# Two products of the MLP's second matrix moved in between the last products of its first, four places for turned blocks, and a reordered second batch

## The chip, the cores and the metric

The kernel runs on one core of a Trainium2 chip. Time is device microseconds of one execution; a kernel's time is the median of its runs. Engines: PE (TensorE, matmuls), DVE (VectorE), ACT (ScalarE), POOL (GpSimd), SP (SyncE, which only issues DMAs here). Every engine works through its own list of instructions in order, and waits on semaphores that the kernel sets by hand.

## The reference

A transformer block with cross attention, B = 4 batches of 512 tokens, D = 512, 16 heads of 32, hidden width 2048, all in fp32:

```python
x = layer_norm(hidden_states, ln1_w, ln1_b)
q = (x @ q_w + q_b); k = (encoder @ k_w + k_b); v = (encoder @ v_w + v_b)   # split into 16 heads
attn = softmax(q k^T * scale)
out = (attn @ v) @ cproj_w + cproj_b
hidden = out + residual
y = layer_norm(hidden, ln2_w, ln2_b)
y = gelu(y @ fc_w + fc_b, approximate=True)
y = y @ proj_w + proj_b
return hidden + y
```

## The kernel before, in words

A product in fp32 precision is made of three matmuls on rounded operands, in `mm3`: every operand is held as a high part (a rounded copy, made by ACT) and a low part (operand less high part, made by DVE or POOL).

The first some 400 us are projections and attention, and the change doesn't touch them. Then comes the MLP, in two halves q = 0 and q = 1, each of two batches (2q and 2q + 1). A half has three stages on PE:

- the **front**: for p = 0 to 7, `fc_first(q, p)` and `fc_second(q, p)`, six matmuls each. `fc_second(q, p)` waits for ACT's `copy_first(q, p)`, which takes the result of `fc_first` out of PSUM. For q = 0 the four blocks `cproj(3, c)` of attention's output projection (twelve matmuls each) stand in the front too;
- the **rest**: for p = 0 to 7, five products `fc_rest(q, p, which)` of six matmuls each, which = 6, 5, 7, 4, 3. They are the seven-product scheme of Strassen and Winograd over the 2 x 2 blocks of batches and halves of the hidden features, so results are put together by additions on DVE: `add_u2` after product 6, `add_u3` after 7, `add_c22` after 5, `add_c21` after 4, `add_c12` after 3. ACT then applies GELU to each with `gelu_rest`;
- the **second product**: `pj(n)`, twelve matmuls for each of 32 features n (32 for each half). Before `pj(n)`, ACT makes the high parts of the weights and of the hidden feature (`second_high(n)`, `hidden_high(n)`), and DVE their low parts (`second_low(n)`, `hidden_low(n)`).

The operands of the rest are prepared during the front. The second batch of a half goes through a normalisation and a turn: DVE turns four 128 x 512 blocks (`y_block(b, c)`) into the tile `turned(b, c)`, SP stores each with four DMAs to the DRAM tensor yt (`y_store`), and loads yt back (`y_load`). Then DVE (`y_affine`) or ACT (`y_scale`) apply weight and bias, DVE forms four differences (`block(q, n)`, 128 x 1024 elements), and five operands YQ[0] to YQ[4] are split: high parts by ACT (`block_high`), low parts by DVE for 0 to 2 (`block_low`) and by POOL for 3 and 4. The weights of the rest ("wr") are loaded, POOL makes their sums (`weight_sums`), ACT their high parts (`rest_high(q, p)`), DVE their low parts (`rest_low(q, p)`). These lie in three places that are used in turn, `rest(q, p)`; `second(n)` shares memory with them.

All orders are written out by hand. In the rest, ACT's and DVE's lists for feature p stand in one loop; for p = 7 they hold `add_c21(7)`, `add_c12(7)` and two `gelu_rest`, and behind the loop the preparation of n = 2, 3 and on. The lines that later parts name: L991 `copy_first`, L994 all GELUs, L1050 and L1052 `rest_high`, L1108 `block_high`, L1061 `second_high`, L1075 `hidden_high`; L1299 `y_affine`, L1295 `y_block`, L1401 `block`, L1405 `block_low`, L1385 and L1388 `rest_low`, L1417 `add_u2`, L1427 `add_u3`, L1440 `add_c21`, L1447 `add_c12`, L1458 `second_low`, L1453 `hidden_low`; L1668 the low parts on POOL; L432 `y_store`, L439 `y_load`, L409 `load_weights` on SP.

## Time and profile before

| | |
|---|---|
| median of 3 runs | 771.61 us (769.97 to 775.69) |
| profiled execution | 771.54 us, of which the span from first to last instruction is 769.7 |
| PE busy | 729.8 us, 95% of the span |
| DVE, ACT, POOL busy | 544.4, 401.5, 351.0 us |
| TensorE clock, mean | 0.993 of full |

The span is nearly all PE. What an engine list or a wait costs is therefore read from PE's idle stretches and from the stretches in which its granted clock is below 1.00, and from what released PE at the end of each idle stretch. Other engines' idle time costs nothing by itself.

### The profile page before, as it was taken

The page shows a single profiled execution, that of the slowest core. Times are in us where ns is not written, and L with a number is a line of the kernel's source. Part 1 is how long each engine was busy: PE and PEld are TensorE (multiplying, and loading weights), DVE is VectorE, ACT ScalarE, POOL GpSimd, SP SyncE. Part 2 cuts the span into 40 slices and gives each one's busy share as a digit, 9 for nine tenths or more (in the row PEclk, how much of TensorE's full clock was granted, in tenths as well). Part 3 has the DMA queues.
Part 4 walks back from the last instruction along what each step waited for, and adds up shares of the span by engine and source line. Part 5 has one row for each costly group of instructions (what it writes and reads, how often), then busy time and mean ns, then how long its engine had stood idle before and what let it go on. Part 6 is the DMA issues. An engine that isn't in the chain of part 4 may idle for free.

```text
span 769.7 us, 10364 instructions
## 1 busy us (share of the span) xinstructions
PE 729.8 (95%) x3568; PEld 497.8 (65%) x3568; DVE 544.4 (71%) x1071; ACT 401.5 (52%) x690; POOL 351.0 (46%) x241
## 2 busy tenths in 40 slices
PE   7999999989999999999999889999999989999998
PEld 5878886733344444344436768778777878868886
DVE  6773347788888888898695857677599457654474
ACT  4434241276766666666684635354556554454442
POOL 2644150078998788798574367000045167000030
PEclk9999999999999999999999989999999999999999
DMA  9756377597666784678836832134883452033362
GB/s 328 236 161 229 127 223 231 196 265 171 157 165 149 187 235 115 173 197 180 228 103 156 259 105 70 40 85 115 212 270 104 118 179 83 27 96 96 95 207 82
DMA packets 118196, 124.24 MB, mean 161 GB/s; under 512 B 41248, under 2 KB 66084, under 8 KB 118144
## 3 DMA queue, kind: packets, MB, share of 16 engines
q1 hardware_dynamic: 91888, 98.39, 45.1%
q10 hardware_dynamic: 26256, 25.19, 11.0%
q8 instruction: 28, 0.46, 0.3%
q14 instruction: 24, 0.20, 0.1%
HBM read 94.05 MB, written 29.37 MB: 160 GB/s over the span
## 4 chain that ended last, share of the span: by engine, by line
PE 75%; DVE 15%; ACT 5%; issue 3%; DMA 1%; SPq 1%; POOL 0%; ACTq 0%; DVEq 0%
PE ps L592 20%; PE ps L594 19%; PE ps L593 19%; DVE ps L1344 7%; PE ps L715 5%; PE ps L699 5%; PE ps L684 4%; PE ps L730 4%; DVE R L1546 2%; ACT Pt L960 1%; DVE BIG L1458 1%; DMA yt<-FU 1%; DVE mx L1344 1%; PE ps L652 1%; DVE R L1276 1%
## 5 line engine op out<-in xcount | busy, mean ns | idle before, releaser
L960 ACT ACTIVATE Pt<-ps 128x512 f32<-128x512 f32 x256 | 137.6, 597 | 72.4 <-PE ps L699 71.5
L699 PE MATMUL ps<-BIG 98*128 98x512 f32 x256 | 92.7, 439 | 3.5 <-ACT Pt L960 3.1
L1344 DVE CUSTOM_DVE_ANT_0 ps<-ps,FU 128x512 f32<-128x512 f32 x128 | 84.6, 722 | 14.9 <-PE ps L684 14.8
L1344 DVE CUSTOM_DVE_ANT_0 ps<-ps,BIG 128x512 f32<-128x512 f32 x128 | 84.6, 723 | 10.9 <-PE ps L684 10.7
L699 PEld LDWEIGHTS ps<-BIG 98*128 98x128 f32 x256 | 44.1, 188 | 67.5 <-issue 28.3
L1458 DVE TENSOR_TENSOR BIG<-RW,BIG 128x512 fp32r<-128x512 f32 x64 | 50.2, 784 | 49.4 <-ACT BIG L1061 49.3
L1061 ACT ACTIVATE BIG<-RW 128x512 fp32r<-128x512 f32 x64 | 40.3, 629 | 80.7 <-PE ps L594 79.8
L592 PE MATMUL ps<-BIG,HR 128*128 128x512 f32 x172 | 68.4, 397 | 5.2 <-DVE HR L1453 5.2
L994 ACT ACTIVATE BF<-BF,cols 128x512 f32<-128x512 f32 x48 | 34.5, 723 | 68.1 <-DVE BF L1447 29.5
L1800 POOL TENSOR_TENSOR R<-Pt 128x1024 f32<-128x1024 f32 x20 | 47.3, 2390 | 46.6 <-ACT Pt L960 46.6
L1739 POOL TENSOR_TENSOR R<-R,cbt 128x512 f32<-128x512 f32 x16 | 26.0, 1652 | 93.2 <-DMA R<-hd 93.2
L715 PE MATMUL ps<-Pt,V 128*32 128x512 f32 x512 | 68.2, 605 | 0.0
L593 PE MATMUL ps<-BIG,HR 128*128 128x512 f32 x172 | 67.5, 393 | 0.0
L594 PE MATMUL ps<-BIG,HR 128*128 128x512 f32 x172 | 67.5, 392 | 0.0
L1668 POOL TENSOR_TENSOR BIG<-R,BIG 128x512 fp32r<-128x512 f32 (+1 forms) x31 | 42.4, 1391 | 45.9 <-ACT BIG L972 27.0
L592 PE MATMUL ps<-BIG 128*128 128x512 f32 x128 | 52.7, 411 | 7.0 <-DVE BIG L1475 5.8
L1331 DVE SCALAR_TENSOR_TENSOR BIG<-ps,cols,BIG 128x512 fp32r<-128x512 f32 x31 | 23.0, 748 | 45.4 <-ACT BIG L942 45.2
L1800 POOL TENSOR_TENSOR RAWY<-Pt 128x1024 f32<-128x1024 f32 x22 | 52.1, 2389 | 3.9 <-ACT Pt L960 3.9
L942 ACT ACTIVATE BIG<-ps,cols 128x512 fp32r<-128x512 f32 x31 | 21.3, 688 | 57.4 <-PE ps L594 57.4
L592 PE MATMUL ps<-BIG,WK 128*128 128x512 f32 x128 | 50.9, 398 | 0.0
L593 PE MATMUL ps<-BIG 128*128 128x512 f32 x128 | 50.8, 397 | 0.0
L594 PE MATMUL ps<-BIG 128*128 128x512 f32 x128 | 50.5, 395 | 0.0
(186 smaller groups left out, 1734.9 us busy)
## 6 DMA issues: line engine op xcount, KB each, us to landing
RW<-in_proj_w ACTq DMA_DIRECT2D x64, 256.0 KB, 2.6
BIG<-qs SPq DMA_DIRECT2D x62, 256.0 KB, 2.8
BIG<-ks SPq DMA_DIRECT2D x62, 256.0 KB, 3.1
ks<-BIG SPq DMA_DIRECT2D x32, 256.0 KB, 2.0
qs<-BIG SPq DMA_DIRECT2D x32, 256.0 KB, 5.5
R<-hd SPq DMA_DIRECT2D x20, 256.0 KB, 4.1
RW<-in_fc_w ACTq DMA_DIRECT2D x20, 256.0 KB, 3.0
R<-in_x SPq DMA_DIRECT2D x16, 256.0 KB, 5.4
```

Of the source, the lines that this page charges most:

```text
L592: eng.matmul(outp, a[0], b[0], start=first, stop=False, skip_group_check=onto)
L593: eng.matmul(outp, a[1], b[0], start=False, stop=False, skip_group_check=onto)
L594: return eng.matmul(outp, a[0], b[1], start=False, stop=last, skip_group_check=onto)
L699: eng.matmul(bk, K_[0:98, j, kc * 128:(kc + 1) * 128], Q_[0:98, j, :], start=True, stop=True).then_inc(S["p_ra"], 1)
L715: ins = eng.matmul(bank(7)[32 * j:32 * j + 32, :], V[:, 4 * b + kc, c:c + 32], Pt[:, r, j % 2, :], start=kc == 0, stop=kc == 3)
L960: eng.activation(Pt[:, r, j % 2, :], bank(bank_a(("s2", i, j))), ACT.Exp, scale=SCALE).then_inc(S["a_ra"], 1)
L994: eng.activation(dst, src, ACT.Gelu_apprx_tanh, bias=fcb[:, f:f + 1]).then_inc(S[done], 1)
L1061: eng.activation(second(n)[0], raw_w(("pj", n, 0)), ACT.Copy).then_inc(S["a_pj"], 1)
L1344: eng.tensor_tensor_reduce(out=scores, in0=scores, in1=MASK[s // 4], scale=1.0, scalar=-3.4e38, op0=ALU.add, op1=ALU.max, accum_out=mx[:, ...
L1458: eng.tensor_tensor(lo, raw_w(("pj", n, 0)), hi.bitcast(F32), ALU.subtract).then_inc(S["v_pj"], 1)
L1668: eng.tensor_tensor(dst, src, high.bitcast(F32), ALU.subtract).then_inc(S[name], 1)
L1800: eng.tensor_tensor(pair(m)[:, 2 * hp:2 * hp + 2, :], Pt[:, (r - 2) % 6, :, :], Pt[:, r, :, :], ALU.add).then_inc(S["g_ac"], 1)
```

## The change

It has five parts.

1. On PE, `pj(32q)` and `pj(32q + 1)` stand inside the last step p = 7 of the rest, where products 6, 5 and 7 of the next feature would stand: `pj(0)` before product 4, `pj(1)` between products 4 and 3. The first feature behind the rest is `pj(2)`. ACT's and DVE's preparation of these two is moved up to step p = 6, and the loads of their weights ahead of that step's GELUs.
2. In the front of q = 0, `cproj(3, 0)` and `cproj(3, 1)` move from step p = 2 to step p = 3.
3. `y_store(1)` and `y_load(1)` go ahead of the loads of wr 0 and wr 1 in SP's list. On DVE `y_affine(1)` and the four `block(0, n)` move up (p = 1 and 2 in place of p = 2, 3 and 4), and ahead of two `front_low_part`; on ACT the `block_high` and `rest_high(0, 0)`, `rest_high(0, 1)` move up.
4. In q = 1 the loads of wr 8 and wr 9 come with steps p = 0 and 1 of the front in place of 3 and 4, and `rest_high(1, 0)`, `rest_high(1, 1)` follow the GELUs of p = 5 and p = 7. `second(n)` for n from 32 on lies in other places.
5. `turned(b, c)` uses four places for batches 1, 2 and 3 (two in FU, two in R0), where batches 2 and 3 used the two of FU. So `y_block(3, c)` waits for the store of block c of batch 2, and no `y_block` waits for a store of its own batch.

```diff
-            return R0[:, c % 2, :] if b == 1 and c >= 2 else FU[:, c % 2, :]
+            return R0[:, c % 2, :] if b and c >= 2 else FU[:, c % 2, :]
...
             load_weights(("wf", 7, 0))
-            for m in range(2):
-                for h in range(2):
-                    load_weights(("wr", m, h))
             for c in range(4):
                 y_store(1, c)
             y_load(1)
-            for h in range(2):
-                load_weights(("wr", 2, h))
+            for m in range(3):
+                for h in range(2):
+                    load_weights(("wr", m, h))
...
+                    if q == 0 and p == 3:
+                        pe.wait_ge("v_rb", NB)
+                        for c in range(2):
+                            cproj(3, c, range(4), bank(c)).then_inc(S["p_cp"], 1)
                     fc_second(q, p)
-                    if q == 0 and 2 <= p < 4:
-                        pe.wait_ge("v_rb", NB)
-                        for c in (2 * p - 4, 2 * p - 3):
+                    if q == 0 and p == 3:
+                        for c in range(2, 4):
                             cproj(3, c, range(4), bank(c)).then_inc(S["p_cp"], 1)
...
                     if p + 1 < HF:
                         fc_rest(q, p + 1, 6)
+                    else:
+                        pj(32 * q)
                     fc_rest(q, p, 4)
                     if p + 1 < HF:
                         fc_rest(q, p + 1, 5)
+                    else:
+                        pj(32 * q + 1)
                     fc_rest(q, p, 3)
                     if p + 1 < HF:
                         fc_rest(q, p + 1, 7)
-                for n in range(32 * q, 32 * q + 32):
+                for n in range(32 * q + 2, 32 * q + 32):
                     pj(n)
...
-                if b == 1 and c >= 2:
-                    dve.wait_ge("p_sm", NS)
-                elif c >= 2:
-                    dve.wait_ge(f"d_ys{c - 2}", 64 * (b + 1))
+                if b == 3:
+                    dve.wait_ge(f"d_ys{c}", 64 * b)
                 elif b == 2:
                     dve.wait_ge("v_wr", 2 * HF)
-                elif b:
-                    dve.wait_ge(f"d_ys{c + 2}", 64 * b)
+                elif b == 1 and c >= 2:
+                    dve.wait_ge("p_sm", NS)
+                elif b == 1:
+                    dve.wait_ge(f"d_ys{c + 2}", 64)
+                elif c >= 2:
+                    dve.wait_ge(f"d_ys{c - 2}", 64)
```

**The end of the rest on ACT.** These are ACT's rows before, from the loads of the weights of `pj(2)` and `pj(3)` on. L994 are GELUs; behind the one that waits for s_v_c12 the second time come `second_high(1)` and `second_high(2)`.

```order
L1081 DMA RW<-in_proj_w 128x512 [waits s_v_wr]
L1081 DMA RW<-in_proj_w 128x512
L994 ACTIVATE BF<-BF,cols 128x512 [waits s_v_c22]
L1061 ACTIVATE BIG<-RW 128x512 [waits s_p_p3,s_d_w0]
L1075 ACTIVATE HR<-BF 128x512 [waits s_a_g11]
L994 ACTIVATE BF<-BF,cols 128x512 [waits s_v_c21]
L994 ACTIVATE BF<-BF,cols 128x512 [waits s_v_c12]
L1061 ACTIVATE BIG<-RW 128x512 [waits s_d_w1]
L1075 ACTIVATE HR<-BF 128x512 [waits s_a_g11]
L1061 ACTIVATE BIG<-RW 128x512 [waits s_d_w2]
L1075 ACTIVATE RX<-BF 128x512 [waits s_a_g11]
```

And after, at the same place:

```order
L1000 ACTIVATE BF<-BF,cols 128x512 [waits s_v_c21]
L1067 ACTIVATE BIG<-RW 128x512 [waits s_p_p3,s_d_w0]
L1081 ACTIVATE HR<-BF 128x512 [waits s_a_g11]
L1000 ACTIVATE BF<-BF,cols 128x512 [waits s_v_c12]
L1000 ACTIVATE BF<-BF,cols 128x512 [waits s_v_c22]
L1067 ACTIVATE BIG<-RW 128x512 [waits s_d_w1]
L1081 ACTIVATE HR<-BF 128x512 [waits s_a_g11]
L1000 ACTIVATE BF<-BF,cols 128x512 [waits s_v_c21]
L1000 ACTIVATE BF<-BF,cols 128x512 [waits s_v_c12]
L1067 ACTIVATE BIG<-RW 128x512 [waits s_d_w2]
L1081 ACTIVATE RX<-BF 128x512 [waits s_a_g11]
```

The preparation of features 0 and 1 moved ahead of the last two GELUs; that of feature 2 (the last two rows) still stands behind both.

**The front of q = 0 on DVE**, before, from the load of batch 1 on:

```order
L1299 TENSOR_SCALAR BF<-BF,cols 128x512 [waits s_d_yl3]
L1379 TENSOR_TENSOR RY<-RW,RY 128x512 [waits s_a_wf]
L1601 TENSOR_TENSOR R<-ps,R 128x512 [waits s_g_xc,s_p_cp] x2
L1401 TENSOR_TENSOR BF<-BF,HN 128x1024 [waits s_p_ra,s_v_ya]
L1401 TENSOR_TENSOR BF<-BF 128x1024 [waits s_v_tt]
L1601 TENSOR_TENSOR R<-ps,R 128x512 [waits s_g_xc,s_p_cp] x2
L1401 TENSOR_TENSOR BF<-BF 128x1024
L1401 TENSOR_TENSOR BF<-HN,BF 128x1024 [waits s_v_tt]
L1405 TENSOR_TENSOR SLX<-BF,SLX 128x1024 [waits s_a_yq] x2
L1385 TENSOR_TENSOR BIG<-V,BIG 128x256 [waits s_a_wr]
L1388 TENSOR_TENSOR BIG<-FU,BIG 128x1024 [waits s_a_wr]
L1405 TENSOR_TENSOR SLX<-BF,SLX 128x1024 [waits s_a_yq]
```

And after:

```order
L1305 TENSOR_SCALAR BF<-BF,cols 128x512 [waits s_d_yl3]
L1407 TENSOR_TENSOR BF<-BF,HN 128x1024 [waits s_p_ra,s_v_ya]
L1407 TENSOR_TENSOR BF<-BF 128x1024 [waits s_v_tt]
L1385 TENSOR_TENSOR RY<-RW,RY 128x512 [waits s_a_wf]
L1407 TENSOR_TENSOR BF<-BF 128x1024
L1407 TENSOR_TENSOR BF<-HN,BF 128x1024 [waits s_v_tt]
L1385 TENSOR_TENSOR RY<-RW,RY 128x512 [waits s_a_wf]
L1610 TENSOR_TENSOR R<-ps,R 128x512 [waits s_g_xc,s_p_cp] x2
L1411 TENSOR_TENSOR SLX<-BF,SLX 128x1024 [waits s_a_yq] x2
L1610 TENSOR_TENSOR R<-ps,R 128x512 [waits s_g_xc,s_p_cp] x2
L1411 TENSOR_TENSOR SLX<-BF,SLX 128x1024 [waits s_a_yq]
L1391 TENSOR_TENSOR BIG<-V,BIG 128x256 [waits s_a_wr]
```

The four differences (L1401, now L1407) moved ahead of the additions of attention's output (L1601, now L1610) and of two low parts of front weights (L1379, now L1385, of which one stood ahead of these rows before).

## Rows read from the trace of the kernel before

**Rows 1.** The page, part 1: busy us, share of the span, instructions.
```profile
PE 729.8 (95%) x3568; PEld 497.8 (65%) x3568; DVE 544.4 (71%) x1071; ACT 401.5 (52%) x690; POOL 351.0 (46%) x241
```

**Rows 2.** PE's waits from 400 us on: total us, times, longest us.
```profile
PE ps L592 <- DVE HR L1453: 5.2, 6, 2.7
PE ps L592 <- DVE BF L1417: 2.8, 1, 2.8
PE ps L592 <- DVE BIG L1388: 2.3, 1, 2.3
PE ps L592 <- ACT BF L991: 1.9, 1, 1.9
PE ps L592 <- DVE BF L1427: 1.6, 2, 0.8
PE ps L592 <- POOL BIG L1668: 1.3, 1, 1.3
```

**Rows 3.** Windows: us, busy of PE, PEld, DVE, ACT, POOL, granted clock, DMA share, GB/s.
```profile
445.00:448.00 3.00, 1.04 (x3) 0.89 (x4) 1.81 (x2) 0.00 (x0) 3.00 (x4) 0.71 0.34 130
448.00:451.00 3.00, 3.00 (x9) 2.35 (x8) 1.00 (x2) 0.00 (x0) 2.92 (x5) 0.50 0.00 0
451.00:454.00 3.00, 3.00 (x10) 2.38 (x9) 1.07 (x2) 1.98 (x3) 0.78 (x2) 0.65 0.48 139
...
559.00:561.00 2.00, 2.00 (x5) 1.61 (x6) 1.95 (x2) 0.91 (x2) 1.54 (x2) 0.50 0.81 177
561.00:563.00 2.00, 2.00 (x8) 1.57 (x7) 2.00 (x3) 0.00 (x0) 1.43 (x1) 0.67 1.18 186
```

**Rows 4.** Timeline of ACT, two features apart by one: start, us, ..., idle before, releaser.
```profile
540.12 0.63 ACT L1061 ACTIVATE BIG<-RW 128x512 fp32r<-128x512 f32 x1 [1.57 <-PE ps L594]
...
542.84 0.63 ACT L1061 ACTIVATE BIG<-RW 128x512 fp32r<-128x512 f32 x1 [1.57 <-PE ps L594]
```

**Rows 5.** Timeline of DVE where the rest of q = 0 ends.
```profile
503.74 0.68 DVE L1447 TENSOR_TENSOR BF<-ps,BF 128x512 f32<-128x512 f32 x1
...
506.35 0.68 DVE L1453 TENSOR_TENSOR HR<-BF,HR 128x512 fp32r<-128x512 f32 x1
```

**Rows 6.** Timeline of ACT at the same place.
```profile
504.48 0.71 ACT L994 ACTIVATE BF<-BF,cols 128x512 f32<-128x512 f32 x1
```

**Rows 7.** Timeline of PE: q = 0's first product 7, and `pj(1)`.
```profile
446.95 0.77 PE L592 MATMUL ps<-SLX,BIG 128*128 128x512 f32 x1 [2.83 <-DVE BF L1417]
...
507.09 0.50 PE L592 MATMUL ps<-BIG,HR 128*128 128x512 f32 x1 [0.81 <-DVE HR L1453]
```

**Rows 8.** Timeline of SP, `y_store(1)` and `y_load(1)`.
```profile
408.67 6.45 SPq L432 DMA_DIRECT2D yt<-FU  x8
415.17 4.40 SPq L432 DMA_DIRECT2D yt<-R  x8
421.07 2.06 SPq L439 DMA_DIRECT2D BF<-yt  x4
```

**Rows 9.** Timeline of DVE in the front of q = 0.
```profile
424.01 2.84 DVE L1299 TENSOR_SCALAR BF<-BF,cols 128x512 f32<-128x512 f32 x3 [6.58 <-DMA BF<-yt]
...
429.45 1.21 DVE L1401 TENSOR_TENSOR BF<-BF,HN 128x1024 f32<-128x1024 f32 x1
...
443.42 2.79 DVE L1388 TENSOR_TENSOR BIG<-R,BIG 128x1024 fp32r<-128x1024 f32 x1 [0.52 <-ACT BIG L1052]
```

**Rows 10.** Timeline of ACT in the front of q = 0: `copy_first(0, 7)`.
```profile
439.09 0.60 ACT L991 ACTIVATE BF<-ps 128x512 f32<-128x512 f32 x1
```

**Rows 11.** Timeline of POOL there: low parts of YQ[3] and YQ[4].
```profile
439.28 5.84 POOL L1668 TENSOR_TENSOR YT<-BF,YT 128x1024 fp32r<-128x1024 f32 x2 [11.83 <-ACT YT L1108]
```

**Rows 12.** Timeline of DVE at the third block of batch 3.
```profile
557.06 0.71 DVE L1295 STREAM_TRANSPOSE FU<-R 128x512 f32<-128x512 f32 x1 [6.82 <-DMA yt<-FU]
```

**Rows 13.** Timeline of ACT at the end of q = 1's front: `rest_high(1, 0)`, `rest_high(1, 1)`.
```profile
618.96 0.42 ACT L1050 ACTIVATE BIG<-V 128x256 fp32r<-128x256 f32 x1 [0.30 <-issue]
...
621.11 1.04 ACT L1052 ACTIVATE BIG<-R 128x1024 fp32r<-128x1024 f32 x1
```

More of the change, by code:

```diff
@@ L110, in second @@
         def second(n):
-            return [BIG[:, 21504 + 1024 * (n % 3) + 512 * h:][:, 0:512] for h in range(2)]
+            base = (21504, 22528, 23552)[n % 3] if n < 32 else (19968, 21504, 18944)[n % 3]
+            return [BIG[:, base + 512 * h:][:, 0:512] for h in range(2)]
         SUMS = [t.rearrange("p a n -> p (a n)") for t in (FU, R0[:, 0:2, :])]
@@ L1220, in _ @@
                             load_weights(("wr", HF * q + p + 4, h))
+                    if 5 <= p < 7:
+                        load_weights(("pj", 32 * q + 2 * p - 10, 0))
+                        load_weights(("pj", 32 * q + 2 * p - 9, 0))
                     gelu_rest(q, p, 21)
+                    if p == 6:
+                        second_high(32 * q)
+                        hidden_high(32 * q)
                     gelu_rest(q, p, 12)
@@ L1230, in _ @@
                     if p == 6:
-                        second_high(32 * q)
-                        hidden_high(32 * q)
-                second_high(32 * q + 1)
-                hidden_high(32 * q + 1)
+                        second_high(32 * q + 1)
+                        hidden_high(32 * q + 1)
                 for n in range(2, 32):
@@ L1593, in _ @@
                         front_low_part(0, p + 4)
-                    if q == 0 and p == 2:
+                    if q == 0 and p == 1:
                         for k in range(4):
                             y_affine(1, k)
+                    if q == 0 and 1 <= p < 3:
+                        block(0, 2 * p - 2)
+                        block(0, 2 * p - 1)
                     if q == 0 and 3 <= p < 5:
@@ L1621, in _ @@
                         rest_low(q, p + 2)
+                    if p == 6:
+                        second_low(32 * q)
+                        hidden_low(32 * q)
                     add_c12(q, p)
@@ L1625, in _ @@
                         add_c22(q, p + 1)
[L1626 to L1628 removed]
+                    if p == 6:
+                        second_low(32 * q + 1)
+                        hidden_low(32 * q + 1)
                 for n in range(2, 32):
```

39 lines of the change are left out of this document (13 added, 26 removed).

## The prediction

> **What bounds the kernel now.** I read the page first: PE is busy for 729.8 of 769.7 us [rows 1]. The change adds no matmul and takes none away, so all it can move is PE's idle time and the stretches at the lower clock. Second, PE's waits in the MLP [rows 2]: they sum to 15.1 us in the six rows (a total of 16.1 with two of 0.6 and 0.4 that are left out). Each row belongs to one place. 1.3 is `cproj(3, 0)` waiting for POOL; 1.9 the last `fc_second` of q = 0 waiting for `copy_first`; 2.8 the first product 7 of the rest waiting for `add_u2`; 2.3 the start of the rest of q = 1 waiting for `rest_low`; 1.6 (twice 0.8) is product 4 of step 7 waiting for `add_u3`; of the 5.2 on `hidden_low`, 2.7 stands at feature 19 of q = 0, and most of the rest at the two hand-overs from the rest to the second product. Third, the granted clock [rows 3]. It is 1.00 but for two stretches: 0.71, 0.50 and 0.65 over 445 to 454 us, and 0.50 and 0.67 over 559 to 563. The lower level is 1.2 GHz, half of 2.4. A mean of 0.71 over 3 us is 1.74 us at half clock, so the first stretch holds 1.74 + 3.0 + 2.1 = 6.8 us, of which PE was busy 1.04 + 3 + 2.1 = 6.1 and lost half, 3.1 us. The second holds 2.0 + 1.3 = 3.3 us and lost 1.7. The first began in the idle of 2.8, the second in that of 2.7; idles of 2.3 and 1.9 had no such stretch. So the whole stock for this change is 16.1 + 3.1 + 1.7 = 20.9 us, 2.7% of the time.
>
> The unit: ACT's step to the next feature is released by PE every 542.84 - 540.12 = 2.72 us [rows 4], so `pj(n)` (twelve matmuls) takes 2.72 us and a product of six 1.36.
>
> **Part 1, `pj` inside the rest (twice, for q = 0 and 1).** What it removes: product 4 of step 7 no longer follows at once on product 7, whose result `add_u3` needs, so the 0.8 goes [rows 2]. The two idles at `pj(0)` and `pj(1)`, 0.3 and 0.8 (the second in [rows 7]), go or shrink: their operands are now made during step 6. Laying the same durations along step 6, I get `hidden_low(1)` some 0.3 us after PE wants `pj(1)`, an estimate. So 1.9 us of idle becomes 0.3.
>
> What it adds: behind product 3 of step 7 there is now nothing ready for PE. `pj(2)` needs `hidden_low(2)`, and this stands behind product 3 in every list: DVE's next is `add_c12(7)`, which reads product 3; ACT's next is the GELU on it; then `second_high(2)`, `hidden_high(2)`, then DVE's two low parts. The trace has the same chain for `pj(1)`: `add_c12` starts at 503.74 [rows 5], its GELU at 504.48 [rows 6], `hidden_low` at 506.35 [rows 5], and PE goes on at 507.09 [rows 7], 3.35 us after the start of the addition. Before, `pj(0)` with its 2.72 us covered most of it. Now nothing does: with some 0.2 us from product to addition PE stands still for 3.35 + 0.2 = 3.55 us (3.4 as the wait view counts, from the drain of the last matmul). Queued behind the waiting instructions are only the preparations of features 3 and on. Balance of one hand-over: each idle costs PE about 0.3 us more than the view counts, for the drain and the slower first matmul (0.50 for some 0.39 [rows 7]). Before, three idles: 1.9 + 0.8 = 2.7. Now two: 3.55 + 0.3 + 0.2 = 4.0. So +1.3 us. Bounds: 0 (if the addition came through at once and `pj(1)` didn't wait) and 2.
>
> Then the clock. An idle of 3.4 us is longer than both that were followed by half clock [rows 2, 3]. What it costs is bounded by 0 (as after 2.3) and by 3.1 us (as after 2.8); between the two stretches of before, 1.7 and 3.1, weighted for a chance that none comes, I take 1.9. Part 1 for both halves: 2 x (1.3 + 1.9) = +6.4 us, ends 0 and +10.
>
> **Part 5, four places.** DVE sat 6.8 us until a store of yt had landed before it could turn the third block of batch 3 [rows 12], and feature 19 waited behind that: 2.7 us idle [rows 2] and 1.7 at half clock. With four places the block waits for a store of batch 2, issued some 10 us earlier. What is late next there? DVE has 3 operations of 0.6 us for a feature of 2.72, and was some 3 us ahead of PE before that wait, so nothing is. Value: -2.7 - 1.7 = -4.4. Ends: -4.5 and -1 (POOL's low parts of batch 2, which slow DVE shortly after, could now catch it there).
>
> **Part 4, the start of q = 1's rest.** PE waited 2.3 us for `rest_low(1, 0)`, behind `rest_high(1, 0)`, which started at 618.96 [rows 13]. The weights are now loaded three steps of 2.72 us earlier and `rest_high(1, 0)` stands behind the GELU of step 5 in place of that of step 6, so this wait goes. But `rest_high(1, 1)` still follows the last GELU: it would end some 0.9 us earlier than the 622.15 of before [rows 13], and `add_u2` stands behind `rest_low(1, 1)` in DVE's list, so product 7, third of the rest, now waits some 1.4 us where it didn't. Value -1.0, ends -1.6 and 0. The moved loads stand ahead of two loads of front weights in ACT's list, which are needed two steps later, 5 us; four issues of some 0.5 us don't use that up.
>
> **Parts 2 and 3, the front of q = 0.** `cproj` behind a product more: the 1.3 us for POOL is hidden [rows 2]. SP issues the stores of yt in 6.45 us for the first eight, with 1 MB of wr ahead of them in the queues, and 4.40 for the next eight [rows 8]. Without it 16 cost 8.8 us and not 10.9, so `y_load(1)` goes out at 418.8 rather than 421.07, and `y_affine` starts near 421.7 rather than 424.01 [rows 9]. The blocks then end at about 431 rather than 435. On ACT three `block_high` fall before `copy_first` of step 7 as before, and `rest_high(0, 1)` (1.3 us) is added before it. I get its start at 438.1 for 439.09 [rows 10], so the last `fc_second` gains 1 us, no more: PE idles 2 us here as before. From there 6, 5 and 7 of step 0 need `rest_low(0, 0)` and `rest_low(0, 1)`. DVE's work from the last `y_affine` (425.1) to `rest_low(0, 1)` is 14.9 us: four `block` and three `block_low` of 1.2 [rows 9], two low parts and four additions of 0.6, two `rest_low` of 1.55. With no disturbance it is done at 440.0, PE flows from 438.8 on, product 7 starts at 442.9 rather than 446.95 [rows 7], and the clock doesn't fall: -4.05 - 3.1 = -7.1 us.
>
> But DVE is disturbed. The `rest_low` at 443.42 took 2.79 us where the same form takes 1.2, and it ended 1.1 us after POOL's second low part, which ended at 445.12 [rows 9, 11]. Before, POOL's two low parts, 2.9 us each, started at 439.28, when DVE had only `rest_low(0, 1)` left. Now `block_high` of YQ[3] ends at 433.5 on ACT, and POOL's 5.8 us fall over `block_low(0, 1)`, `block_low(0, 2)` and `rest_low(0, 0)`; its weight sums fall over the blocks. Each such meeting cost DVE 1.6 us in the row, and four to five of them make DVE 3 to 7 us late: product 6 starts at 441.5 to 445, product 7 at 444.3 to 447.8. I take 445.0, -2.0 us. PE then idles 2 us before the last `fc_second` and about as much before product 6, which makes the lower clock likely again: of the 3.1 us I count one back. Value -3.0; ends -7.1 and +3 (product 7 at 447.8 and 2 us more at half clock).
>
> The Trainium skill, page "SBUF — State Buffer", section "Who interferes with whom" and the diagram's reading before it, calls the port that VectorE and GpSimd share an exclusive lock, held for the whole instruction when the VectorE operation has two SBUF inputs. The row at 443.42 agrees. By the rule every low part and block here waits for a whole POOL instruction, by a sharing of bandwidth it would be slower by a part; the first gives the later end of my range for this part, the second about -5.
>
> **Sum.** +6.4 - 4.4 - 1.0 - 3.0 = -2.0 us on the profiled execution's 771.54 us (span 769.7 and 1.8 around it), which stands at the median, 771.61. Forecast: 769.5 us.
>
> **Rivals.** A: DVE isn't held up by POOL in the front. For it: 0.6 us operations pass between POOL's in many places. Against: the row of 2.79. Then the front gives -7.1: 771.5 + 6.4 - 4.4 - 1.0 - 7.1 = 765.4. B: the idle of 3.4 us leaves the clock alone, as 2.3 did; with the rest as forecast 769.5 - 3.8 = 765.7, and with A 761.6. Against it speak both stretches of [rows 3]. C, slower: DVE's lateness in the front. If `rest_low(0, 0)` comes later than 444, product 7 of step 0 starts later than before and PE's idle before product 6 is over 3 us, with half clock behind it: +3 there, and with both hand-overs at the 3.1 us price (2 x 4.4 = +8.8) the sum is +3 + 8.8 - 4.4 - 1.0 = +6.4, 777.9 us. It decides from about two meetings of DVE and POOL of full length more than I count. D: the hand-over costs nothing because the chain is shorter than in [rows 5 to 7]; I see no instruction that leaves it. It would give 769.5 - 6.4 = 763.1.
>
> **How the numbers follow.** Forecast 0.50, A 0.17, B 0.12, C 0.13, D and mishaps 0.08. Measurement can tell about 1%, 7.7 us. Range: 763 to 776, the forecast's own being 766.5 to 772.5. Faster by over 1% (below 763.9) needs A with B, or D: 0.19. Slower by over 1% (above 779.3) needs more than C: 0.06. Within: 0.75.
>
> **What would show it.** Right: PE idle of about 3.4 us before `pj(2)` and `pj(34)`, released by `hidden_low`; no wait of DVE on a store of yt near 557; a short wait at product 7 of q = 1. In the front, the start of product 7 of step 0 against 446.95 tells A, the forecast and C apart, and the length of DVE's L1411 and L1394 tells whether POOL is the cause. The granted clock behind each hand-over tells B. I am wrong if the hand-over shows under 2 us of idle, or if the third block of batch 3 still holds DVE.

## The result, and the profile after

The changed kernel takes 777.19 us (median of 13 runs, 774.32 to 780.06), the kernel before beside it 771.88 (13 runs). The ratio is 1.0067, with a 95% interval of 1.0047 to 1.0087: some 5.2 us slower. The forecast was 769.5 with a range of 763 to 776, and 777.19 lies above it. It lies 0.7 us from rival C's 777.9; whether C was right is taken up near the end.

The profiled execution of the changed kernel took 780.01 us (span 778.2, mean clock 0.987), 2.8 above its median, so its rows show more loss than the runs do. The line of the page that answers [rows 1]:

```profile
PE 734.9 (94%) x3568; PEld 501.5 (64%) x3568; DVE 548.2 (70%) x1071; ACT 401.5 (52%) x690; POOL 354.9 (46%) x241
```

The same 3568 matmuls take 5.1 us more, nearly all of it clock (worked out below), and PE's idle time rises from 39.9 to 43.3 us. PE's waits from 400 us on (total, times, longest), to set beside [rows 2]:

```profile
PE ps L591 <- DVE HR L1459: 5.6, 3, 3.4
PE ps L591 <- DVE BIG L1394: 3.8, 1, 3.8
PE ps L591 <- DVE RX L1459: 3.4, 1, 3.4
PE ps L591 <- ACT BF L997: 3.3, 2, 2.9
PE ps L591 <- DVE BF L1423: 1.3, 1, 1.3
PE ps L591 <- DVE RY L1385: 1.2, 1, 1.2
```

18.6 us in six rows, for 15.1 before. PE's timeline says where each stands (in brackets the idle time before the row):

```profile
442.01 0.50 PE L591 MATMUL ps<-YT,RY 128*128 128x512 f32 x1 [2.87 <-ACT BF L997]
447.45 0.79 PE L591 MATMUL ps<-SLX,BIG 128*128 128x512 f32 x1 [3.79 <-DVE BIG L1394]
...
512.97 0.79 PE L591 MATMUL ps<-BIG,RX 128*128 128x512 f32 x1 [3.38 <-DVE RX L1459]
...
586.54 0.50 PE L591 MATMUL ps<-BIG,HR 128*128 128x512 f32 x1 [1.96 <-DVE HR L1459]
...
628.97 0.47 PE L591 MATMUL ps<-SLX,BIG 128*128 128x512 f32 x1 [1.26 <-DVE BF L1423]
...
690.18 0.79 PE L591 MATMUL ps<-BIG,HR 128*128 128x512 f32 x1 [3.39 <-DVE HR L1459]
```

In order: the last `fc_second` of q = 0; product 6 of its rest, which waits for `rest_low(0, 0)`, where before product 6 went through and product 7 waited [rows 7]; `pj(2)`; `pj(27)`; product 7 of q = 1; `pj(34)`. The last row of the wait view, 1.2 us, is new and not in the forecast: at 435.89 us PE waits for a low part of the front's weights (L1385), ahead of which part 3 had put DVE's differences. The wait at feature 19 [rows 2] is gone, as is the 2.3 us before the rest of q = 1. A first matmul of 0.79 us in place of 0.50 ran at half clock already: the clock had fallen inside the idle. Windows of the two hand-overs (the seventh number is the granted clock):

```profile
513.00:516.00 3.00, 3.00 (x7) 2.42 (x8) 3.00 (x6) 1.28 (x3) 0.00 (x0) 0.50 0.32 109
516.00:519.00 3.00, 3.00 (x9) 2.28 (x9) 1.11 (x2) 0.45 (x1) 0.00 (x0) 0.53 0.00 0
...
693.00:696.00 3.00, 3.00 (x9) 2.33 (x8) 0.00 (x0) 0.24 (x1) 0.00 (x0) 0.50 0.00 0
```

Read in short windows, the clock stood at 1.2 GHz for 20.5 us: 6.8 at each hand-over (from 512.0 and 689.5, 1.0 and 0.7 us before the idle ended), 3.4 from 447.1, 3.4 from 587.1. Before it was 10.2 us [rows 3]. Half clock costs only while PE works: it was busy in 18.5 of the 20.5 us, and in 9.5 of the 10.2 before. Half of the difference is 4.5 us, most of the 5.1 by which PE's busy time grew.

**A ledger.** Taking the starts of the same DVE instruction in both profiles and subtracting gives the place of each loss. The first row is noise: attention has the same code in both, and over all twenty profiles of this study that point lay anywhere within 2.3 us.

| stretch | shift, us | forecast |
|---|---|---|
| up to 404 us, code unchanged | +0.9 | |
| front of q = 0, to `add_c12(0)` | +0.9 | -3.0 |
| first hand-over, to feature 8 | +4.0 | +3.2 |
| features 19 to 22 (four places) | -4.6 | -4.4 |
| features 22 to 28 | +3.4 | 0 |
| start of q = 1's rest | -0.2 | -1.0 |
| second hand-over, to feature 40 | +4.1 | +3.2 |
| all | +8.5 | -2.0 |

So the two hand-overs came as forecast or dearer, the four places gave what was forecast and lost most of it a few features later, and the front lost where it should have gained. One profile can't settle terms of one or two us, since half clock comes and goes between executions; the runs below can.

### The profile page after: what moved, and what is told of

It reads as the page before. It is cut to its first block, busy times and chain, and to the rows that moved or that the text cites. A ratio compares the mean times of both kernels' runs of the same rounds, so it can differ in the third digit from the quotient of the medians.

```text
span 778.2 us, 10363 instructions
## 1 busy us (share of the span) xinstructions
PE 734.9 (94%) x3568; PEld 501.5 (64%) x3568; DVE 548.2 (70%) x1071; ACT 401.5 (52%) x690; POOL 354.9 (46%) x241
## 4 chain that ended last, share of the span: by engine, by line
PE 73%; DVE 15%; ACT 4%; issue 3%; DMA 2%; SPq 1%; POOL 1%; ACTq 0%; DVEq 0%
PE ps L591 19%; PE ps L593 19%; PE ps L592 19%; DVE ps L1350 5%; PE ps L698 4%; PE ps L714 4%; PE ps L683 4%; PE ps L729 3%; DVE R L1552 2%; ACT Pt L966 1%; SPq L433 1%; DVE BF L1407 1%; DMA qs<-BIG 1%; PE ps L651 1%; DVE mx L1350 1%
## 5 line engine op out<-in xcount | busy, mean ns | idle before, releaser
L1350 DVE CUSTOM_DVE_ANT_0 ps<-ps,FU 128x512 f32<-128x512 f32 x128 | 84.6, 724 | 15.2 <-PE ps L683 15.1
L591 PE MATMUL ps<-BIG,HR 128*128 128x512 f32 x172 | 69.6, 405 | 5.8 <-DVE HR L1459 5.6
L593 PE MATMUL ps<-BIG,HR 128*128 128x512 f32 x172 | 68.7, 399 | 0.0
L592 PE MATMUL ps<-BIG,HR 128*128 128x512 f32 x172 | 68.7, 399 | 0.0
L1808 POOL TENSOR_TENSOR R<-Pt 128x1024 f32<-128x1024 f32 x20 | 47.3, 2386 | 45.8 <-ACT Pt L966 45.8
L1676 POOL TENSOR_TENSOR BIG<-R,BIG 128x512 fp32r<-128x512 f32 (+1 forms) x31 | 42.3, 1382 | 46.4 <-ACT BIG L978 27.0
L1337 DVE SCALAR_TENSOR_TENSOR BIG<-ps,cols,BIG 128x512 fp32r<-128x512 f32 x31 | 23.0, 749 | 45.9 <-ACT BIG L948 45.8
```

What stands on the lines that cost most here:

```text
L591: eng.matmul(outp, a[0], b[0], start=first, stop=False, skip_group_check=onto)
L592: eng.matmul(outp, a[1], b[0], start=False, stop=False, skip_group_check=onto)
L593: return eng.matmul(outp, a[0], b[1], start=False, stop=last, skip_group_check=onto)
L1350: eng.tensor_tensor_reduce(out=scores, in0=scores, in1=MASK[s // 4], scale=1.0, scalar=-3.4e38, op0=ALU.add, op1=ALU.max, accum_out=mx[:, ...
L1676: eng.tensor_tensor(dst, src, high.bitcast(F32), ALU.subtract).then_inc(S[name], 1)
L1808: eng.tensor_tensor(pair(m)[:, 2 * hp:2 * hp + 2, :], Pt[:, (r - 2) % 6, :, :], Pt[:, r, :, :], ALU.add).then_inc(S["g_ac"], 1)
```

## Each part by itself

Where the runs allow, a part is priced by its ratio to the kernel before, timed on the same chip.

**Part 1 taken out (e1).** The changed kernel with both preparations and both products back in their old places:

```diff
-                    else:
-                        pj(32 * q)
...
-                    else:
-                        pj(32 * q + 1)
...
-                for n in range(32 * q + 2, 32 * q + 32):
+                for n in range(32 * q, 32 * q + 32):
```

> The changed kernel without part 1: products pj(0), pj(1), pj(32), pj(33) and their preparation stand where they stood before, parts 2 to 5 stay. Theory H (the hand-over from the rest to the second product costs about 4 us each time, 1.3 of stall and nearly 3 of half clock, and parts 2 to 5 together are worth about nothing): 769 to 772 us, 0.997 to 1.001 of the kernel before, no idle over 2 us of PE at either hand-over. Rival P (only the stall, 1.3 us twice, belongs to the hand-over; the rest of the loss comes from parts 2 to 5): 774 to 775 us, 1.003 to 1.005.

771.47 us, ratio 0.9997 (0.998 to 1.0014). Theory H holds: what was lost goes away with part 1, and parts 2 to 5, forecast at -8.4 us together, are worth 0.2, give or take 1.3.

**Part 1 alone (e2)**, the opposite edit on the kernel before.

> The kernel before with part 1 alone (and the other places of second(n) in q = 1, which part 1 needs there). Theory H: PE idle of 3.4 us in front of pj(2) and pj(34), each with some 6.8 us at half clock behind it, 777 to 780 us, 1.006 to 1.010 of the kernel before. Rival P (stall alone): 774 to 775 us, 1.003 to 1.005.

777.76 us, ratio 1.0081 (1.0055 to 1.0106), +6.3 us; the forecast's term was +6.4. Its timeline of PE has both idles:

```profile
509.74 0.80 PE L593 MATMUL ps<-BIG,RX 128*128 128x512 f32 x1 [3.39 <-DVE RX L1459]
...
689.38 0.50 PE L593 MATMUL ps<-BIG,HR 128*128 128x512 f32 x1 [3.39 <-DVE HR L1459]
```

Half clock followed both here too, 3.4 us each, not 6.8 as in the changed kernel's profile and as the expectation had it.

**Part 5 alone (e3)**:

```diff
-            return R0[:, c % 2, :] if b == 1 and c >= 2 else FU[:, c % 2, :]
+            return R0[:, c % 2, :] if b and c >= 2 else FU[:, c % 2, :]
...
```

(The part left out is DVE's new waits, as in the diff ahead of the prediction.)

> The kernel before with part 5 alone. Theory G (most of the gain is given back a few features later, since the load of batch 3's yt comes no earlier and ACT's y_scale(3) stands ahead of second_high(24)): the idle of 2.7 us before pj(19) goes and another of 1.5 to 3 us comes at pj(24) or pj(25); 769.5 to 771.5 us, 0.997 to 1.000. Rival (the prediction's part 5, nothing is late next): 767.2 us, 0.994, and no idle between pj(16) and pj(26).

772.26 us, ratio 1.0001 (0.9982 to 1.0019): nothing of the 4.4 us. PE's idle at feature 19 is gone, and `pj(22)`, counted from the start of `pj(8)`, comes 4.5 us earlier, here and in every kernel of the study that has part 5. So the forecast's gain was there; but two other idles stand behind it, at features 24 and 27:

```profile
571.42 0.50 PE L592 MATMUL ps<-BIG,HR 128*128 128x512 f32 x1 [1.78 <-DVE HR L1455]
...
581.84 0.50 PE L592 MATMUL ps<-BIG,HR 128*128 128x512 f32 x1 [1.95 <-DVE HR L1455]
```

SP's and ACT's timelines say why for the first. SP of the kernel before, then of e3:

```profile
548.98 13.09 SPq L432 DMA_DIRECT2D yt<-FU  x16
563.86 2.70 SPq L439 DMA_DIRECT2D R<-yt  x4
```

```profile
548.87 7.23 SPq L432 DMA_DIRECT2D yt<-FU  x8
556.14 6.15 SPq L432 DMA_DIRECT2D yt<-R  x8
565.35 1.76 SPq L439 DMA_DIRECT2D R<-yt  x4
```

The blocks are turned earlier (the third at 549.85, before at 557.06), but SP still needs 13.4 us to issue their sixteen stores and the load goes out no sooner. Why SP takes as long when nothing waits for the blocks stays open. So ACT, now ahead by the 4.5 us gained, waits for that load, with `second_high(24)` behind it in its list. ACT's row in the kernel before, then in e3:

```profile
568.01 1.52 ACT L1085 ACTIVATE R<-R,cols 128x512 f32<-128x512 f32 x2 [0.45 <-DMA R<-yt]
```

```profile
568.00 1.52 ACT L1085 ACTIVATE R<-R,cols 128x512 f32<-128x512 f32 x2 [5.26 <-DMA R<-yt]
```

The same instruction starts at the same time in both; before, it had 0.45 us to wait, and that was all the room that there was. The second idle, at feature 27, falls together with POOL's `bias_add`; e14 and e17 below take it up.

**Parts 2 and 3 alone (e4)**, the edits as in the diff ahead of the prediction.

> The kernel before with parts 2 and 3 alone (the front of q = 0). Theory F (what the earlier blocks gain is lost to the meetings of DVE with POOL and to the later weights): product 7 of step 0 starts at 446 to 449 us, where it was 446.95, and the time is 771 to 773.5 us, 0.999 to 1.002. Rival (the prediction's parts 2 and 3): 768.8 us, 0.996, product 7 at 445.

772.63 us, ratio 1.0015 (0.9996 to 1.0034), +1.2 us. The rival, the forecast's own -3.0, is out. The time came as theory F had it, the place did not: what starts at 446.3 is product 6, and product 7, expected at 446 to 449, came at 450.4.

**Part 4 alone (e9)**:

```diff
-                    if q and 3 <= p < 5:
+                    if q and p < 2:
...
-                    if q and p == 6:
+                    if q and p == 5:
                         rest_high(1, 0)
```

> The kernel before with part 4 alone (and the other places of second(n) in q = 1). Theory Q (the idle of 2.3 us at the start of q = 1's rest goes, one of 1.3 us comes at product 7, and the half clock that followed the longer idle in five of seven profiles goes with it): 769 to 771 us, 0.997 to 0.999 of the kernel before. Rival (the prediction's 1.0 us is all given back at product 7): 771.5 us, 1.000.

769.93 us, ratio 0.9983 (0.9965 to 1.0002), -1.3 us, forecast -1.0. The interval leaves out a gain over 2.7 us, not zero. Over all profiles of the study, half clock followed the idle of 2.3 to 3.0 us at this place in 8 of 13 kernels without part 4, and the idle of 1.2 to 1.8 in none of 7 with it. The stall itself hardly shrank: from the start of the front of q = 1 to product 5 of step 2 of its rest PE takes 38.0 us in e9, and 38.05 in the kernel before, whose profile has no half clock there. Over the seven kernels with part 4 it is 37.7 to 38.1, but for e18; over the five without it whose profiles have no half clock at the start of the rest, 38.05 to 38.8. So by the profiles part 4 is worth some 0.4 us of stall, and the rest of the 1.3 is half clock that comes less often.

The four measured prices, +6.3, +0.1, +1.2 and -1.3, sum to +6.3 us, against 5.2 measured for the whole, which is within their intervals (each is 1.4 to 2 us either way).

## Why the hand-over costs that

**e5, one product inside, one behind product 3:**

```diff
                     if p + 1 < HF:
                         fc_rest(q, p + 1, 5)
-                    else:
-                        pj(32 * q + 1)
...
-                for n in range(32 * q + 2, 32 * q + 32):
+                for n in range(32 * q + 1, 32 * q + 32):
```

> The kernel before with part 1 changed: only pj(0) and pj(32) stand inside the rest, pj(1) and pj(33) follow product 3; the preparation of both is early as in part 1. Theory H (the chain from product 3 to hidden_low(2), 3.55 us, has nothing in front of it in part 1): the 2.72 us of pj(1) stand over it, the idle before pj(2) is 0.7 to 1.0 us, the idles before product 4, pj(0) and pj(1) are gone, no half clock at either hand-over; 768 to 770 us, 0.996 to 0.998 of the kernel before. Rival L (the early preparation on ACT and DVE is what costs, by delaying the GELUs and additions): 774 us or more, like part 1 alone.

767.45 us, ratio 0.9942 (0.9928 to 0.9957), a little better than even theory H had it. From e2 this is one product of each half moved by one place, and some 10 us less. PE's idle before `pj(2)` is what the chain is longer than `pj(1)`:

```profile
506.97 0.50 PE L593 MATMUL ps<-BIG,RX 128*128 128x512 f32 x1 [0.67 <-DVE RX L1457]
```

3.39 - 2.72 = 0.67 to the hundredth, and no half clock followed either hand-over.

**e6, the preparations early, PE's order as before** (both products behind product 3).

> The kernel before with ACT's and DVE's lists of part 1, while PE keeps its old order (all products pj behind product 3). Theory H: the idles before pj(0) and pj(1) go (0.3 and 0.8 us with the drain, twice), that of 0.8 before product 4 stays: 769 to 770.5 us, 0.997 to 0.999. Rival L (the lists are what costs): 774 us or more.

768.56 us, ratio 0.9952 (0.9935 to 0.9969), again below the case of theory H. The early lists cost nothing, they are the gain of part 1; rival L is out. With the same lists of ACT and DVE, e2, e5 and e6 differ only in which products PE has left when product 3 is done, and that is what costs.

**e7, stall against clock** (an edit of e2):

```diff
+                for _ in range(2):
+                    product(bank(FRONT_BANKS[q][0]), [x[:, 0:256] for x in rest(q, 7)], YQ[4], (0, 1), True)
                 for n in range(32 * q + 2, 32 * q + 32):
```

> The kernel before with part 1, and behind each product 3 of step 7 twelve more matmuls, 2.72 us, whose operands are ready and whose result nobody reads (a repetition of product 3 into a free bank), so that PE stands still for some 0.7 us in place of 3.4. The time to pj(2) is the same. Theory C (the clock falls because PE stands still, and that is the larger half of the hand-over's cost): no half clock behind either hand-over, 773.5 to 775.5 us, where part 1 alone gave 777.8. Rival S (the stall is the whole cost, the half clock would come somewhere in any case): 777 to 778.5 us.

775.35 us, ratio 1.0048 (1.0031 to 1.0064), 2.4 us under e2, though it does more work and `pj(2)` waits for the same chain. Its windows at the hand-overs:

```profile
509.00:512.00 3.00, 2.79 (x12) 2.30 (x13) 3.00 (x6) 1.43 (x3) 0.00 (x0) 1.00 0.46 130
688.00:691.00 3.00, 2.89 (x12) 2.36 (x13) 2.46 (x5) 1.41 (x3) 0.00 (x0) 1.00 0.33 120
```

Theory C holds in direction: without the half clock the same stall costs less. By the medians, 2.4 of the 6.3 us are clock and 3.9 are left for the stall, but other stretches of these runs vary too. The traces price the hand-over alone. This is PE's time in us from the start of product 5 of step 6 to the start of `pj(8)`, in q = 0 and in q = 1:

| kernel | q = 0 | q = 1 | half clock there |
|---|---|---|---|
| before | 38.2 | 38.2 | none |
| changed | 42.2 | 42.3 | 6.8 us each |
| e2, part 1 alone | 40.8 | 41.1 | 3.4 us each |
| e7, with filler | 39.5 | 39.5 | none |
| e5, one product inside | 36.3 | 36.3 | none |
| e6, lists alone | 36.5 | 36.5 | none |

So the stall of one hand-over is 39.5 - 38.2 = 1.3 us, 2.5 for both, which is the forecast's figure. The clock adds 1.3 and 1.6 us in e2's profile, and 2.7 and 2.8 in the changed kernel's. Of the 6.3 us of e2 the hand-overs show 5.4 in the profile; the remaining 0.9 is not placed.

## Why the front lost

The changed kernel's timelines of DVE, then POOL, before the wait of 3.79 us at product 6:

```profile
436.86 2.94 DVE L1411 TENSOR_TENSOR SLX<-BF,SLX 128x1024 fp32r<-128x1024 f32 x2
...
440.92 2.86 DVE L1411 TENSOR_TENSOR SLX<-BF,SLX 128x1024 fp32r<-128x1024 f32 x1
443.71 2.56 DVE L1391 TENSOR_TENSOR BIG<-V,BIG 128x256 fp32r<-128x256 f32 x1
446.19 1.21 DVE L1394 TENSOR_TENSOR BIG<-FU,BIG 128x1024 fp32r<-128x1024 f32 x1
```

```profile
428.90 1.79 POOL L1736 TENSOR_TENSOR FU<-V 128x256 f32<-128x256 f32 x1 [7.37 <-DMA V<-in_fc_w]
...
440.35 5.63 POOL L1676 TENSOR_TENSOR YT<-BF,YT 128x1024 fp32r<-128x1024 f32 x2
```

`block_low(0, 2)` takes 2.86 us where it took 1.2, and the 256 columns of `rest_low` 2.56 where they took 0.4, each beside one of POOL's two operations of 2.8. That is rival C's mechanism. Over the whole front, DVE's operations up to `rest_low(0, 0)` are some 6.6 us longer than the same forms where they were undisturbed. There is a second suspect: POOL's weight sums start at 428.90, for 421.15 before, since their weights now come behind yt, and so they fall over two of the four differences (1.76 us each in place of 1.2). e10 and e11 take one each away from e4.

**e10, weights loaded as early as before:**

```diff
+            for m in range(2):
+                for h in range(2):
+                    load_weights(("wr", m, h))
             for c in range(4):
                 y_store(1, c)
             y_load(1)
-            for m in range(3):
-                for h in range(2):
-                    load_weights(("wr", m, h))
+            for h in range(2):
+                load_weights(("wr", 2, h))
```

> Parts 2 and 3, but SP's list as before: the loads of wr 0 and wr 1 ahead of the stores of yt. Theory W (the late weights put POOL's weight sums, 421 to 427 before, over DVE's four differences and push all that follows): the sums stand at 421 to 427 again and the differences take 1.2 us each, product 6 of step 0 starts at 443 to 444.5 in place of 446.3, 769.5 to 771.5 us. Rival Y (the earlier y_load is what parts 2 and 3 live on, and the low parts of YQ[3] and YQ[4] on POOL are what holds DVE): no earlier than with parts 2 and 3 whole, 772 to 774 us.

773.12 us, ratio 1.0031 (1.0012 to 1.005), and product 6 at 446.29: theory W falls. The sums stood at 422 to 428.7 and the differences took 1.2 us again, but POOL, free sooner, now did its low parts beside `block_low(0, 0)` and `block_low(0, 1)` (DVE's row, then POOL's):

```profile
436.13 6.31 DVE L1409 TENSOR_TENSOR SLX<-BF,SLX 128x1024 fp32r<-128x1024 f32 x2
```

```profile
435.66 2.39 POOL L1671 TENSOR_TENSOR YT<-BF,YT 128x1024 fp32r<-128x1024 f32 x1 [6.93 <-ACT YT L1111]
```

6.31 us for what takes 2.35 alone.

**e11, POOL's low parts one step later:**

```diff
-                if q == 0:
-                    for n in (3, 4):
-                        block_low(0, n)
                 for p in range(HF):
                     if p + 2 < HF:
                         weight_sums(q, p + 2)
+                    if q == 0 and p == 0:
+                        for n in (3, 4):
+                            block_low(0, n)
```

> Parts 2 and 3, with POOL's low parts of YQ[3] and YQ[4] behind its weight sums of step 2 in place of ahead of them (nothing else moves). Theory Y (POOL's two operations of 2.9 us hold DVE's block_low(0, 2) and rest_low(0, 0), 2.9 and 2.6 us in place of 1.2 and 0.4): these two take 1.2 and 0.4 us, product 6 of step 0 starts at 442.5 to 443.5 in place of 446.3, 768.5 to 770.5 us. Rival W (the late weights and their sums set the time): product 6 after 445, 772 to 773.5 us.

768.65 us, ratio 0.9972 (0.9955 to 0.9988): theory Y holds. Product 6 starts at 443.85 with no wait of PE at all, and DVE's two operations are short:

```profile
440.04 1.21 DVE L1407 TENSOR_TENSOR SLX<-BF,SLX 128x1024 fp32r<-128x1024 f32 x1
441.17 0.41 DVE L1387 TENSOR_TENSOR BIG<-V,BIG 128x256 fp32r<-128x256 f32 x1
```

**e13, the same move on the kernel before** (its new front left out), as a control.

> The kernel before with nothing but POOL's low parts of YQ[3] and YQ[4] behind its weight sums of step 2, as in e11. Theory Y (the new front brings the meetings of DVE and POOL; before there was one, at rest_low(0, 1), 1.6 us): product 7 of step 0 starts some 1 us earlier, and at most 1.5 us come of it: 770 to 771.5 us, 0.998 to 1.000. Rival (the gain of e11 is a gain of this order alone, and the new front costs the same with it or without it): 767 to 768.5 us, 0.994 to 0.996.

771.45 us, ratio 0.9989 (0.9967 to 1.0012), in theory Y's case; the rival's 0.994 to 0.996 is out. By the ratios the move takes 3.3 us off the new front (1.0015 to 0.9972) and 0.8 off the old one. The difference of the two, 2.5 us, is about as large as its uncertainty, so the medians alone don't settle it. The traces say what the move frees: two operations of DVE in e11, 2.86 and 2.56 us before it, and one here, `rest_low(0, 1)`, 2.79 us in [rows 9]:

```profile
443.95 1.23 DVE L1388 TENSOR_TENSOR BIG<-R,BIG 128x1024 fp32r<-128x1024 f32 x1 [0.48 <-ACT BIG L1052]
```

Counted from the first matmul of the MLP, product 7 of step 0 starts after 44.4 to 45.8 us in the eleven kernels with the old front and POOL's old order, after 46.3 to 48.3 in the four with the new front and POOL's low parts ahead of its sums, and after 42.9 to 43.5 in the three with the new front and POOL's low parts later. With the old front and POOL's low parts later it is 42.9 here and 45.0 in e16. The forecast's 445.0 is 42.5 on this count. So the new front does bring the meetings, and without those at `block_low(0, 2)` and `rest_low(0, 0)` it comes to about the place that was forecast; but the old front came there too in this run.

## Where the four places' gain goes

**e8, `y_scale(3)` and the differences one feature later:**

```diff
-                        for b, at in ((2, 19), (3, 23)):
+                        for b, at in ((2, 19), (3, 24)):
...
-                        if 25 <= n < 29:
-                            block(1, n - 25)
+                        if 26 <= n < 30:
+                            block(1, n - 26)
```

> The kernel before with part 5, and y_scale(3) one feature later on ACT (behind features 24 and 25), block(1, n) one feature later on DVE (26 to 29). Theory G (the gain of part 5 is given back because y_scale(3), which waits for the load of yt, stands ahead of second_high(24)): PE idle of under 1 us in all between pj(16) and pj(31), 766.5 to 768.5 us, 0.994 to 0.996. Rival (what takes the gain is the contention of POOL's bias_add and the DMAs, wherever y_scale stands): 770.5 to 772 us and still some 3 us of idle there.

770.36 us, ratio 0.9982 (0.9961 to 1.0003). Both half right. No idle over 0.5 us up to feature 30, as G said; then 2.3 us of idle and 1.7 of half clock went at feature 31, where DVE's `hidden_low` met POOL's low parts of YQ[3] and YQ[4] (PE, DVE, POOL in turn):

```profile
592.91 0.58 PE L592 MATMUL ps<-BIG,HR 128*128 128x512 f32 x1 [2.29 <-DVE HR L1455]
```

```profile
590.01 2.85 DVE L1455 TENSOR_TENSOR HR<-BF,HR 128x512 fp32r<-128x512 f32 x1
```

```profile
589.48 2.81 POOL L1670 TENSOR_TENSOR YT<-R,YT 128x1024 fp32r<-128x1024 f32 x1
```

**e14, that meeting moved away too** (the last two high parts, which release POOL, behind feature 31):

```diff
-                        if 27 <= n:
+                        if 27 <= n < 30:
                             block_high(1, n - 27)
+                        if n == 31:
+                            block_high(1, 3)
+                            block_high(1, 4)
```

> The kernel before with part 5, y_scale(3) and the differences of q = 1 one feature later (as in e8) and the high parts of YQ[3] and YQ[4] of q = 1 behind feature 31 (as in e12). Theory G (both give-backs are gone): 767.5 to 769.5 us, 0.995 to 0.997. Rival (POOL's bias_add and low parts hold DVE for as long wherever they stand, and the gain is lost again): 770 to 771.5 us, as e8.

770.02 us, ratio 0.9979 (0.9957 to 1.0), at the near edge of the rival's case. Feature 31 is clear, and 2.38 us of idle stand at feature 28, where POOL's four `bias_add` (573.67 to 580.6) hold DVE:

```profile
575.44 2.31 DVE L1406 TENSOR_TENSOR BF<-R,BF 128x1024 f32<-128x1024 f32 x1
577.67 1.78 DVE L1463 TENSOR_TENSOR BIG<-RW,BIG 128x512 fp32r<-128x512 f32 x1
579.38 1.75 DVE L1458 TENSOR_TENSOR HR<-BF,HR 128x512 fp32r<-128x512 f32 x1
```

**e17, `bias_add(1)` behind POOL's low parts:**

```diff
                     for n in (3, 4):
                         block_low(1, n)
+                    bias_add(1)
...
-                bias_add(2 * q + 1)
+                if q:
+                    bias_add(3)
```

> The kernel of e14 with POOL's bias_add(1) behind its low parts of YQ[3] and YQ[4] of q = 1. Theory G (POOL's additions are the last give-back of part 5): no operation of DVE over 1.3 us and no PE idle over 1 us between features 19 and 31; the whole 4.4 us come through: 767 to 768.5 us, 0.994 to 0.996 of the kernel before. Rival (the additions now hold DVE in q = 1's front and cost the same there): 769.5 to 771 us.

770.88 us, ratio 0.9998 (0.9979 to 1.0018): the rival. Features 19 to 31 are clean (one idle of 0.56 us), and the additions hold DVE in the front of q = 1 for more than they did before (PE, DVE, POOL):

```profile
601.66 0.76 PE L592 MATMUL ps<-YT,BIG 128*128 128x512 f32 x1 [3.64 <-DVE BIG L1384]
```

```profile
586.76 6.04 DVE L1384 TENSOR_TENSOR BIG<-RW,BIG 128x512 fp32r<-128x512 f32 x3 [1.64 <-ACT BIG L1035]
592.72 6.78 DVE L1410 TENSOR_TENSOR SLX<-BF,SLX 128x1024 fp32r<-128x1024 f32 x3
```

```profile
590.51 7.91 POOL L1744 TENSOR_TENSOR R<-R,cbt 128x512 f32<-128x512 f32 x4
```

So in e3, e8, e14 and e17 no more than 1.6 us of the gain at feature 19 reach the end (ratios 0.9979 to 1.0001). The idle there gave DVE, ACT and SP time in which they caught up with q = 1's preparation; without it the same work is late at a later place, and each of these moves moved the place. That isn't so in every arrangement: in the profiles of e12 and e16 below, which have e14's order with one product inside and part 4, `pj(31)` comes 3.8 and 4.2 us earlier than before, counted from `pj(8)`, and the front of q = 1 gives none of it back. Why POOL's additions cost 2.38 us of idle in e14, 1.40 in e12 and 0.5 in e16, with the same order of the lists at that place, stays open.

## The corrected parts together

**e12**: one product inside (e5), part 4, part 5 with the moves of e8 and e14, front as before.

> The kernel before with pj(0) and pj(32) alone inside the rest (as in e5), part 4, and part 5 with y_scale(3) and the differences of q = 1 one feature later (as in e8) and the high parts of YQ[3] and YQ[4] of q = 1 behind feature 31, so that POOL's low parts, which held DVE at feature 31 in e8, come after it. Front of q = 0 as before. If the gains add (4.3 of e5, 1 to 2 of part 4, 3 to 4.4 of part 5): 762 to 765 us, 0.988 to 0.992. Rival (what part 5 gains is taken elsewhere before q = 1's front ends, as twice now): 766 to 767 us.

764.82 us, ratio 0.992 (0.9905 to 0.9935): the top of the first case. **e16** adds POOL's order of e11 to it.

> The kernel of e12 with POOL's low parts of q = 0 behind the sums of step 2, front of q = 0 otherwise as before. Theory Y (parts 2 and 3 are worth something once POOL is out of DVE's way): 763.5 to 765 us, 1 us or more above e15. Rival (parts 2 and 3 are worth nothing in any case): the same as e15 within 0.7 us.

764.75 us, ratio 0.9905 (0.9872 to 0.9937), inside its case. POOL's low parts still met `rest_low(0, 1)` here, unlike in e13:

```profile
443.64 3.34 DVE L1397 TENSOR_TENSOR BIG<-R,BIG 128x1024 fp32r<-128x1024 f32 x1
```

**e15** has parts 2 and 3 too, so it is the changed kernel with three corrections.

> The changed kernel with three corrections: pj(1) and pj(33) behind product 3 (e5), POOL's low parts of q = 0 behind the sums of step 2 (e11), and y_scale(3), the differences and the last two high parts of q = 1 later (e12). If the parts add up: 764.8 less 2.8 of e11, 761 to 763 us, 0.987 to 0.989 of the kernel before. Rival (the front's gain is made of clock and doesn't add): 764 to 766 us.

761.64 us, ratio 0.986 (0.9835 to 0.9885), the best of the study, 3.1 us below e16. With POOL's low parts later, the new front seems to pay; the two intervals still overlap a little, and part of the gap may be that meeting in e16. In e15's profile, 763.64 us, the clock never falls from 400 us to the end of PE's work, and PE is busy for less than in [rows 1]:

```profile
PE 725.7 (95%) x3568; PEld 494.7 (65%) x3568; DVE 545.3 (72%) x1071; ACT 401.3 (53%) x690; POOL 356.2 (47%) x241
```

**e18** moves `bias_add(1)` in e15 as e17 did.

> The kernel of e15 with the same move of bias_add(1). In e15 three idles of 1.2 to 1.5 us stood at features 23 to 27. Theory G: they go, 758 to 760 us, 0.981 to 0.984. Rival: 761 to 763 us.

764.79 us, ratio 0.9915 (0.9887 to 0.9943): neither case, and by the ratios 4 us worse than e15. The three idles, which stood at features 25, 27 and 28, went as theory G said, and the idle of 3.64 us of e17 stands in the front of q = 1. The order of e15 stays.

## Why the prediction was wrong, by its own steps

- **Part 1, +6.4: right.** 6.3 measured (e2), with the idle of 3.4 us and the chain as laid out from [rows 5 to 7]; the stall is 1.3 us for each hand-over, as forecast (e7). The clock, forecast at 1.9 each, was 1.3 and 1.6 in e2's profile and 2.7 and 2.8 in the changed kernel's. Rivals B and D are out: half clock followed both idles in both kernels that have part 1 whole and nothing in the idle.
- **Part 5, -4.4: wrong, and the first of two steps that turned the sign.** The step that failed is "What is late next there? ... so nothing is". It looked at DVE's lead over PE two features ahead, and not at the next wait for a DMA in the lists, ACT's `y_scale(3)` on the load of yt, which had 0.45 us to wait already, nor at POOL's `bias_add`. The gain itself came in full at feature 19 (-4.6), and 3.4 of it went by feature 28. The near end of its range, -1, was not far enough; the measured price is +0.1 (e3).
- **Parts 2 and 3, -3.0: wrong, the other step.** The step that failed is how late DVE would be. The forecast counted four to five meetings of DVE and POOL at 1.6 us each, which is 6.4 to 8.0, put them at 3 to 7, and took a value near the early end ("I take 445.0"). DVE's rows in the changed kernel are 6.6 us longer, and product 6 came at 447.45 for the 442.3 implied. It also had `copy_first(0, 7)` gain 1 us, where it lost 1.4 in the changed kernel's profile and 0.2 in e4's (attention's shift taken off); it missed the new wait of 1.2 us for a front weight, and that the late weights put POOL's sums over two of the differences. Its earlier `y_load(1)` was sound: counted from the MLP's first matmul, it went out after 16.1 to 17.6 us in the six kernels that have part 3 whole, for 18.5 before, where 16.3 was forecast. Measured +1.2 (e4), between the forecast and rival C's +3; C's mechanism is what e11 shows.
- **Part 4, -1.0: near in size (-1.3), and partly by luck.** The new wait at product 7 came (1.26 us for 1.4), but by the profiles the stall shrank by some 0.4 us only, and most of what e9 gained is half clock, which this term didn't count.
- **Rival C's total, 777.9, is near 777.19 by luck.** It took part 5 at -4.4 and part 4 at -1.0 as the forecast did; its +3 for the front and +8.8 for the hand-overs were 1.8 and 2.5 us above what e4 and e2 gave, and so made up for the 4.5 us that part 5 didn't bring.
- **The range** ended at 776, though rival C, at 0.13, stood above it. With -4.4 and -3.0 both at zero the sum is 776.9. Both errors are of one kind, what the other engines do to each other and wait for once their work comes earlier; the sum had no case in which both terms were lost together.
- A small sum was off: the durations listed for DVE's work from 425.1 us on add up to 15.1 us, not 14.9. Nothing hangs on it.

The exclusive lock that the Trainium skill, page "SBUF — State Buffer", section "Who interferes with whom", describes agrees with e10's trace: 6.31 us for two operations of 1.2 beside POOL's two of 2.4. The end of the range that the prediction drew from that rule, +3, was nearer to the measured +1.2 of the front than its own -3.0 was.

## What to carry to other kernels

When an idle of the busiest engine is removed, write down, for each other engine's list, the next wait on a DMA or on another engine after that place, and by how much it is early now. In e3 the next one had nothing to spare, and the whole gain went; no run here shows that the smallest of these sets the gain in general. When a product is pulled ahead of the end of a phase, keep behind that end as much ready work as the chain to the next operand is long: one product of 2.72 us in each half, placed one step later, was worth some 10 us here. Two engines that slow each other want their long operations laid side by side on one timeline before either is moved.
